# First layer's picked experts taken in groups of four tiles, two groups interleaved, with the slot numbers converted by ScalarE, the scan's carry kept by VectorE and one residual buffer

## The reference

```python
def step(S, inps):
    rt, kt, vt, dt = inps
    kv = kt[..., :, None] * vt[..., None, :]
    o = jnp.einsum('bhk,bhkv->bhv', rt, S + u[None, :, :, None] * kv)
    S = dt[..., None] * S + kv
    return (S, o)
...
x = x + jax.nn.gelu(h2 @ ffn_w1, approximate=False) @ ffn_w2
```

## Time and profile before

| what | value |
|---|---|
| median of three runs | 5259.96 us (5259.64 to 5265.22) |
| the profiled execution, its own time | 5266.02 us |
| its span, first to last instruction | 5263.9 us |
| mean granted TensorE clock | 0.887 |
| PE, DVE, POOL, ACT busy | 79%, 69%, 66%, 52% of the span |
| first layer's scan, first and last step start | 49.9 and 2421.5 us |
| picked tiles, first and last gated copy | 513.6 and 2816.9 us |

### The profile page before, as it was taken

The page is one execution under the profiler, slowest core; times in us unless marked ns, Lnnn a source line. Parts: engine busy times, 40 slices in busy tenths (PEclk is TensorE's granted clock), DMA queues, the critical chain, the costliest instruction groups (busy, mean ns, idle before and its releaser), DMA issues. The chain is left out here.

```text
span 5263.9 us, 65583 instructions
## 1 busy us (share of the span) xinstructions
PE 4148.2 (79%) x18979; PEld 2796.2 (53%) x18979; DVE 3655.8 (69%) x6255; ACT 2757.0 (52%) x5922; POOL 3461.1 (66%) x2696
## 2 busy tenths in 40 slices
PE   5777777887777887777665988988888888669994
PEld 1344554554445554455443655555555555458883
DVE  6887578567884668743101998888888889745676
ACT  1333543444335443345533877777777777435552
POOL 3456766566566565675245888888888888745552
PEclk7888878998788988888877999999999999789997
DMA  5224444434534435543275122111221122296787
GB/s 177 87 98 132 134 125 133 134 124 124 131 126 129 129 119 128 152 140 121 70 149 130 51 80 79 69 64 66 97 71 67 66 80 79 79 252 221 240 279 274
DMA packets 377824, 658.44 MB, mean 125 GB/s; under 512 B 43456, under 2 KB 234688, under 8 KB 367136
## 3 DMA queue, kind: packets, MB, share of 16 engines
q1 hardware_dynamic: 240192, 415.02, 24.1%
q0 software_dynamic: 89616, 190.40, 13.0%
q10 hardware_dynamic: 47664, 48.83, 3.4%
HBM read 454.55 MB, written 249.59 MB: 134 GB/s over the span
## 5 line engine op out<-in xcount | busy, mean ns | idle before, releaser
L1656 POOL TENSOR_TENSOR c_dbx<-c_dtx,c_Brep 128x1024 f32<-128x1024 f32 x512 | 1201.4, 2362 | 184.9 <-DVE c_hs L1674 100.2
L1674 DVE TENSOR_TENSOR_SCAN c_hs<-psum,c_carry,c_dbx 128x512 f32<-128x512 f32 x768 | 937.3, 1266 | 119.7 <-ACT psum L1663 70.4
L1094 DVE TENSOR_TENSOR_SCAN a_S<-a_decay,a_carry,a_kv 128x513 f32<-128x513 f32 x512 | 764.9, 1494 | 350.7 <-ACT a_carry L1106 223.1
L1085 POOL TENSOR_TENSOR a_kv<-a_rk,a_kv 128x512 f32<-128x512 f32 x512 | 723.2, 1416 | 405.5 <-DMA a_kv<-v_rows 391.6
L1663 ACT ACTIVATE psum<-c_dt,c_cols 128x512 f32<-128x512 f32 x1024 | 697.4, 688 | 366.0 <-DVE c_hs L1674 360.1
L917 POOL DMA_INDIRECT picked_results<-a_t_y,a_to_slot x331 | 374.4, 1131 | 525.8 <-ACT a_t_hT L933 329.5
L1690 PE MATMUL psum<-ident,c_hs 128*128 128x128 f32 x4096 | 609.7, 282 | 111.0 <-DVE c_hs L1674 106.2
L1690 PEld LDWEIGHTS psum<-ident,c_hs 128*128 128x128 f32 x4096 | 486.1, 144 | 395.0 <-DVE c_hs L1674 216.5
L1100 DVE TENSOR_TENSOR a_prod<-a_rk,a_S 128x512 f32<-128x512 f32 x512 | 465.6, 910 | 46.7 <-PE psum L1116 46.6
L2079 POOL DMA_INDIRECT results<-d_ys,d_to_row x320 | 310.7, 971 | 243.5 <-issue 145.1
L976 PE MATMUL psum<-a_W_down,a_t_hT 128*128 x662 | 268.5, 493 | 191.4 <-ACT a_t_hT L933 170.5
(11 more groups left out here) (314 smaller groups left out, 8446.8 us busy)
## 6 DMA issues: line engine op xcount, KB each, us to landing
a_kv<-v_rows SPq DMA_DIRECT2D x512, 256.0 KB
c_Brep<-b_rows SPq DMA_DIRECT2D x64, 1024.0 KB, 4.8
a_t_rows<-picked_rows ACTq DMA_DIRECT2D x331, 144.0 KB
d_xs<-sorted_rows SPq DMA_DIRECT2D x320, 128.5 KB
x<-picked_results POOLq DMA_DIRECT2D x64, 512.0 KB
d_w<-results SPq DMA_DIRECT2D x64, 512.0 KB, 11.4
d_w<-in_d_experts SPq DMA_DIRECT2D x32, 768.0 KB
picked_rows<-in_picked_pad SPq DMA_DIRECT2D x80, 144.0 KB
```

The source lines that it names most:

```text
L1085: m_kv[g] = pool.mark(nc.gpsimd.tensor_tensor(kv[:, g % NV, 1:C + 1], rk[slot][:, 1, hb, :], kv[:, g % NV, 1:C + 1], ALU.mult))
L1094: m_scan[q] = dve.mark(nc.vector.tensor_tensor_scan(S[:, q % NS, :], decay[cq % 2][:, hb, :], kv[:, q % NV, :], carry[:, sq_:sq_ + 1], ALU ...
L1656: m_dbx[g] = m_dbx[g + 1] = pool.mark(nc.gpsimd.tensor_tensor(dbx[:, r:r + 2, :], dtx[slot][:, e, :].unsqueeze(1).broadcast_to([P, 2, C]), ...
L1674: m_scan[q] = dve.mark(nc.vector.tensor_tensor_scan(hs[:, q % NR, :], psum[:, DA + q % ND, :], dbx[:, q % NX, :], first, ALU.mult, ALU.add))
```

## The change

A turn of `tiles` now handles a group of four tiles in six pieces with `rest(1)` between them. Two groups are in work: the new one is transposed and sent through up and Gelu while the old one goes through its transpose, down and gate. Each of t_xT, t_hT and t_h holds four tiles, and ScalarE moves 512 columns at once. Gates and slots are first copied to `t_of`, so that t_rows is free after the transposes; ScalarE converts the slot numbers to integers. There are 16 padding tiles per segment for 15, so that the tiles divide by four: 336. The carry copy goes from ScalarE to VectorE. `xb`, `to_row` and their semaphores are single, and `attention_out(c)` waits until chunk c-1 is out. Unused small buffers go.

```diff
-        s_xb, s_store, s_rows = ([sem(f"{n}{i}") for i in range(2)] for n in ("xb", "store", "rows"))
+        s_xb, s_store, s_rows = sem("xb"), sem("store"), [sem(f"rows{i}") for i in range(2)]
...
-        xb = [sb(f"xb{i}", [P, TL, D]) for i in range(2)]
+        xb = sb("xb", [P, TL, D])
-        NTX, NTT, NTH, NTY, NTI = 6, 2, 2, 4, 4
+        NTX, NTY = 6, 4
...
-        t_rows, t_xT = sb("t_rows", [P, NTX, Z.width]), sb("t_xT", [P, NTT, D])
-        t_h, t_hT, t_y = sb("t_h", [P, NTH, P]), sb("t_hT", [P, NTH, P]), sb("t_y", [P, NTY, D])
+        t_rows, t_xT, t_of = sb("t_rows", [P, NTX, Z.width]), sb("t_xT", [P, 4, D]), sb("t_of", [P, 2, 4, 2 * E])
+        t_h, t_hT, t_y = sb("t_h", [P, 4, P]), sb("t_hT", [P, 4, P]), sb("t_y", [P, NTY, D])
...
         def load_xb(c):
 
-            slot = c % 2
-            if c >= 2:
-                sp.engine.wait_ge(s_store[slot], 16 * (c // 2))
-            nc.sync.dma_start(xb[slot][:, :, :], chunk_of(chunks_in, c)).then_inc(s_xb[slot], 16)
+            if c >= 1:
+                sp.engine.wait_ge(s_store, 16 * c)
+            nc.sync.dma_start(xb[:, :, :], chunk_of(chunks_in, c)).then_inc(s_xb, 16)
...
-            while c >= 2 and not is_done(("out", c - 2)):
+            while c >= 1 and not is_done(("out", c - 1)):
                 yield
             load_xb(c)
...
-                    act.after(m_T.get(q - NTX), m_ty.get(q - NTX), m_slot.get(q - NTX))
+                    act.after(m_T.get((q - NTX) // 2), m_of.get((q - NTX) // 2))
                     nc.scalar.dma_start(t_rows[:, q % NTX, :], row_of[bass.ds(at_row.pop(j), 1), :, :].rearrange("a p d -> p (a d)")).then_inc(s_tx[q % NTX], 16)
 
+                def transpose_rows(j):
+
+                    q = begun + j
+                    i, bank = yield from G.claim(pe)
+                    for k in range(2):
+                        pe.engine.wait_ge(s_tx[(q + k) % NTX], 16 * ((q + k) // NTX + 1))
+                        for kb in range(KB):
+                            m = nc.tensor.transpose(bank[:, k * D + kb * P:k * D + (kb + 1) * P], t_rows[:, (q + k) % NTX, kb * P:(kb + 1) * P], ident[:, :])
+                    Columns.sent += 2 * KB * P
+                    m_T[q // 2] = pe.mark(m)
+                    return i, bank
+
+                def keep_rows(j, i, bank):
+
+                    q = begun + j
+                    at, side = j % 4, q // 4 % 2
+                    act.after(m_T[q // 2], m_up.get(q // 4 - 1))
+                    m_xT[q // 2] = G.freed[i] = act.mark(nc.scalar.copy(t_xT[:, at:at + 2, :].rearrange("p k d -> p (k d)"), bank))
+                    act.after(m_y.get(q // 2 - 4))
+                    m_of[q // 2] = act.mark(nc.scalar.copy(t_of[:, side, at:at + 2, :], t_rows[:, q % NTX:q % NTX + 2, D:]))
+
+                def down(j):
+
+                    q = begun + j
+                    i, bank = yield from G.claim(pe)
+                    pe.after(m_hT[q // 4])
+                    for k in range(2):
+                        m = nc.tensor.matmul(bank[:, k * D:(k + 1) * D], t_hT[:, j % 4 + k, :], down_flat[:, bass.ds(at_e.pop(j + k) + SH * D, D)], start=True, stop=True)
+                    Columns.sent += 4 * D
+                    m_dn[q // 2] = pe.mark(m)
+                    return i, bank
+
+                def gated(j, i, bank):
+
+                    q = begun + j
+                    if j % 4 == 0:
+                        for k, v in enumerate(numbers(table, NT + j, nc.scalar.engine, E - 1)):
+                            at_gate[j + k] = v
+                    act.after(m_dn[q // 2])
+                    for k in range(2):
+                        if q + k >= NTY:
+                            act.engine.wait_ge(s_ty[(q + k) % NTY], 16 * ((q + k) // NTY))
+                        act.mark(nc.scalar.copy(to_slot[:, (q + k) % NTY:(q + k) % NTY + 1], t_of[:, q // 4 % 2, j % 4 + k, E:][:, bass.ds(at_gate[j + k], 1)]))
+                        m = act.mark(nc.scalar.activation(t_y[:, (q + k) % NTY, :], bank[:, k * D:(k + 1) * D], ACT.Copy,
+                                                          scale=t_of[:, q // 4 % 2, j % 4 + k, :][:, bass.ds(at_gate.pop(j + k), 1)]))
+                    m_y[q // 2] = G.freed[i] = m
...
                 def store(j):
 
                     q = begun + j
-                    pool.after_alone(m_ty[q], m_slot[q])
...
+                    pool.after_alone(m_y[q // 2])
+                    for k in range(2):
+                        nc.gpsimd.indirect_dma_start(out=picked_results[slot], in_=t_y[:, (q + k) % NTY, :], in_offset=None,
+                                                     out_offset=bass.IndirectOffsetOnAxis(ap=to_slot[:, (q + k) % NTY:(q + k) % NTY + 1], axis=0),
+                                                     bounds_check=Z.results - 1).then_inc(s_ty[(q + k) % NTY], 16)
+
+                for j in range(4):
                     fetch(j)
...
-                for step in range(total + 6):
...
-                        store(step - 5)
...
-                        fetch(step + 2)
...
+                held = None
+                for g in range(groups + 2):
+                    q, new, old, older = begun + 4 * g, g < groups, 1 <= g <= groups, g >= 2
+                    if older:
+                        gated(4 * g - 6, *held)
+                    if new:
+                        rows_bank = yield from transpose_rows(4 * g)
+                    yield from rest(1)
+                    if new:
+                        keep_rows(4 * g, *rows_bank)
+                        for k in range(4, 6):
+                            if 4 * g + k < total:
+                                fetch(4 * g + k)
+                    if older:
+                        store(4 * g - 8)
+                    if old:
                         i, bank = yield from G.claim(pe)
...
+                        pe.after(m_h[q // 4 - 1])
+                        for k in range(4):
+                            m = nc.tensor.transpose(bank[:, k * P:(k + 1) * P], t_h[:, k, :], ident[:, :])
+                        Columns.sent += 4 * P
+                        m_hx[q // 4 - 1] = pe.mark(m)
+                    yield from rest(1)
+                    if old:
+                        act.after(m_hx[q // 4 - 1], m_dn.get(q // 2 - 3))
+                        m_hT[q // 4 - 1] = G.freed[i] = act.mark(nc.scalar.copy(t_hT[:, :, :].rearrange("p k d -> p (k d)"), bank))
+                    if new:
+                        rows_bank = yield from transpose_rows(4 * g + 2)
+                    yield from rest(1)
+                    if new:
+                        keep_rows(4 * g + 2, *rows_bank)
+                        for k in range(6, 8):
+                            if 4 * g + k < total:
+                                fetch(4 * g + k)
+                    if older:
+                        store(4 * g - 6)
+                    if old:
+                        held = yield from down(4 * g - 4)
+                    yield from rest(1)
+                    if old:
+                        gated(4 * g - 4, *held)
+                    if new:
+                        for k, v in enumerate(numbers(table, 4 * g, nc.tensor.engine, (E - 1) * KB * P)):
+                            at_e[4 * g + k] = v
                         i, bank = yield from G.claim(pe)
...
-                        m_slot[q - 3] = pool.mark(nc.gpsimd.tensor_copy(to_slot[:, (q - 3) % NTI:(q - 3) % NTI + 1], t_rows[:, (q - 3) % NTX, E:][:, bass.ds(at_slot.pop(j), 1)]))
...
-                        m_ty[q - 3] = G.freed[i] = act.mark(nc.scalar.activation(t_y[:, (q - 3) % NTY, :], bank[:, 0:D], ACT.Copy,
...
+                        pe.after(m_xT[q // 2], m_xT[q // 2 + 1])
+                        for k in range(4):
+                            for kb in range(KB):
+                                m = nc.tensor.matmul(bank[:, k * P:(k + 1) * P], t_xT[:, k, kb * P:(kb + 1) * P], up_flat[:, bass.ds(at_e[4 * g + k] + (SH * KB + kb) * P, P)],
+                                                     start=(kb == 0), stop=(kb == KB - 1))
+                        Columns.sent += 8 * KB * 200
+                        m_up[q // 4] = pe.mark(m)
+                    yield from rest(1)
+                    if new:
+                        act.after(m_up[q // 4], m_hx.get(q // 4 - 1))
+                        m_h[q // 4] = G.freed[i] = act.mark(nc.scalar.activation(t_h[:, :, :].rearrange("p k d -> p (k d)"), bank, ACT.Gelu))
                     if old:
+                        held = yield from down(4 * g - 2)
+                    yield from rest(1)
...
-                    act.after(m_scan[q])
-                    m_kept[q] = act.mark(nc.scalar.copy(carry[:, q % steps - 3:q % steps + 1], S[:, q % NS - 3:q % NS + 1, C]))
+                    dve.after(m_scan[q])
+                    m_kept[q] = dve.mark(nc.vector.tensor_copy(carry[:, q % steps - 3:q % steps + 1], S[:, q % NS - 3:q % NS + 1, C]))
...
```

(2 more changed lines are left out.)

109 lines of the change are left out of this document (19 added, 90 removed).

## The result

The changed kernel took 5099.05 us (median of 4 runs, 5096.82 to 5105.43). The kernel before, on the same chip, took 5262.59 (4 runs, 5259.64 to 5280.81). The ratio is 0.9684 [0.966, 0.9708]: 3.2% faster, 163 us. The profiled execution took 5105.4, its span is 5103.6, 160.3 less than the 5263.9 of before; the sum had forecast -157.

What follows compares the result with a forecast made beforehand. No engine is full; bunched tiles wait in a ScalarE-TensorE loop, which also delays the scan. Terms -115 - 30 - 10 - 8 + 2 + 4 = -157 take 5266 to 5109, as a median said as 5105; eight in ten 5010 to 5225.

Steps and rivals of the forecast that it cites:

- the likeliest case: The forecast itself, the whole kernel at 5105 us, chance 0.60, own range 5045 to 5170.
- (a): Groups of four under the scan hide the ScalarE-TensorE wait: 55% of 212 us, -115, bounds 0 and -212.
- The last segment: 64 tiles behind the scan at 2.1 us each, 140 us against 171: -30, bounds -55 and +8.
- (b): Slot casts from POOL to ScalarE: booked inside (a); without ScalarE idle time as cover, 0.3 us per tile, 73 us.
- (c): Carry copy from ScalarE to VectorE removes the scan's waits for it: -10, bounds +8 and -36.
- (d): 25 tiles between scan's end and last segment get cheaper, some done before: -8, bounds 0 and -40.
- (f): One residual buffer, its load waiting on SP for the store: +2 under the scan, +2 behind it.
- rival A: Waits only change owner; where tiles run alone ScalarE sets the pace: 5205 us, chance 0.20.
- (e): Five more tiles, 336 for 331, four of them under the scan: +2.
- B: Everything bound by tiles goes: 5010 us, chance 0.10.
- C: The single residual buffer becomes the cycle, stores and dense layer slip under the scan: slower, 5360 us, chance 0.06.
- D: The change doesn't act: tiles stay bunched, VectorE's copies eat the carry's gain: 5260 us, chance 0.04.

## Why the prediction was right, and where its steps were not

The direction, the size and the likeliest case held: 5099 against 5105, in a range of 5010 to 5225. But the sum came out by terms that were off on both sides: 44 us too little gain under the scan; 29 too much behind it, 6 too much in the last segment, and 6 that came in the untouched rest. That they cancelled is luck; 15 of the 29 are the idle stretch of one execution, and the other three runs of the changed kernel are 5 to 9 us shorter than the profiled one.

**(a) Groups, under the scan: mechanism right, size a little low.** It took 55% of 212 us of tile cost, -115. With chunk 9 as the base on both sides the cost fell from 239 us (13 chunks, 2011 less 13 x 136.3) to 90, -150; with each kernel's own tile-free chunks as base, from 212 to 90, -122. So 58 to 63% went. In the bunched steps of chunk 7 13.1 us of 26.5 went, with 16 tiles for 19, and not the 18 of the working; what made up for it lies in steps 28 to 31, which the prediction did not look at: steps 12 to 31 of chunk 7 against chunk 9 cost 8.3 us before and 2.0 now. The run with one group at a time shows that the wait between ScalarE and TensorE, which the prediction named as the price, is what the interleaving takes out: 4.3 us of 9.1 per group there, 1.8 of 7.04 here.

**The base fell too.** Tile-free chunks took 138.3 in the mean before; chunk 9 is now 134.7 (forecast 137). Part of that is scatter: the single-edit versions have such chunks at 133 to 139. This is the rest of the -165.

**The last segment: -24 for -30, by another cause.** The pace of 2.1 per tile was put down to idle between ScalarE and TensorE. The loop is faster than that, 1.76 per tile where nothing else waits, and its floor was set too high: 1.73 came from adding durations that overlap. What costs is the store wait of 53 us, a buffer cycle through POOL, which the prediction had written down only as "POOL's wait". Where it is gone, the segment takes 113.3, 57 us less than before, just past the term's bound of -55.

**(b) The slot casts: the sum was booked inside (a), the condition was not.** "0.3 us per tile shows in full if the cover is gone" is what the cast alone showed in its sign (+0.45%); with groups the move is worth 39 us. The prediction had POOL on the path only where it holds the scan back, and there it shows: the wait for a_kv is 246 us with the casts on POOL and 158 without.

**(c) The carry copy: -10 forecast, 0 measured**, and +4 in the three first chunks, by the copies' own duration. The prediction halved the gain because the a_kv rows or TensorE's sums are late next. They are, and they take all of it.

**(d) The stretch behind the scan: the step that failed.** "Each gets cheaper and some are done before: -8", with (f) -6; measured +23.4, and +6 to +8 without the idle stretch of that execution. The sign is wrong either way: 30 tiles lay there for 25, not fewer, and the pieces wait out three turns each where no scan step comes. The segment's last tile comes at 186.1 us behind the scan's last product (199.5 in the profiled execution) instead of 178.2, and the plan of the last segment waits for its store. The prediction's own rival A names the three turns, but reads them as a pace that is too fast under the scan, and they were too slow behind it. One turn there brings the stretch to 212.3 us, 12 below the kernel before.

**(e) and (f)** are within their size. One buffer is worth nothing; the waits on SP that were priced at +4 exist (11.2 us behind the scan) and are covered.

**The rivals.** A was right for the carry and wrong for the total: ScalarE's work per tile was not the pace, it had 1.8 us of waits for TensorE left in each group. B's 5010 was reached only by other edits (5002). C fell with the total and with the loads, which slip in four chunks and catch up; its two signs, later loads and a longer stretch behind the scan, were both seen in part, the second for the reason under (d). D fell with the windows. Of what would show it: eight of twelve tile chunks lie within 141 to 154 us and four below, the tile-free one at 134.7 for 137; the last tiles took 146 for 140; the 0.16 us copies, the slot copies at 0.19 and the absent carry wait were as said; POOL's wait ahead of the stores was not (128.3 us for t_y under the scan, for under 100); nor the clock, 0.86 in the bunched steps with TensorE busy for 44.7 of 63.2 us, where over 0.90 was forecast. In the steps behind them it is 0.96 with 76.7 of 86.9. The direction is that of the Trainium skill, "TensorE: Matmul & The Clock Gate", "What's actually happening", by which activity releases the throttle. The bunched steps came out faster at the same clock, 0.86 for 0.85, with TensorE busy for 71% of them where it had been 70%.

## What to carry to other kernels

A wait that leads the list is worth at most what the next late thing leaves of it: take the second and third of the same engine before you book the first, and book nothing where they are nearly as long. Where work is emitted by turns, read every pause at the place where its clock has stopped (here behind the scan, where a rest became three turns), and look for who waits for the last of the work (the next plan). Price a queue by what stands behind a waiting instruction: the same cast cost 0.45% before the groups and brought 0.75% after them.

## What the runs showed that was not expected

A conversion of a single column (128x1) to int32 takes 173 to 210 ns on ScalarE, a copy of 128x64 from SBUF 242 to 292, a copy of 128x512 from PSUM 580 to 590. By durations, a group's two t_xT copies, its t_hT copy and its Gelu take 0.59 x 3 + 0.60 = 2.4 us, where four tiles took (0.38 + 0.27 + 0.30) x 4 = 3.8: 1.4 saved. Four slot copies and two t_of copies add 4 x 0.19 + 2 x 0.26 = 1.3. As said in the prediction, ScalarE got no lighter; what the groups save is trips. The scan itself lasts longer in the grouped kernels, 1559 ns in the mean for 1494, 33 us over 512 of them; with the carry back on ScalarE it is 1570, with the slot casts back on POOL 1511. Why, no run shows.

```profile
L952 ACT CAST a_to_slot<-a_t_of x336: 173/190/210, 527.9 to 2650.6; 128x1 int32 x168
L929 ACT COPY a_t_of<-a_t_rows x168: 242/258/292, 514.2 to 2641.2; 128x64 f32<-128x64 f32 x168
```

And the scan's end and the total are not the same goal: the version with the earliest scan end (2182.0) is slower than four that end it 31 to 98 us later.
